# A language-model block on one core: another bracketing across chunks, the vector engine's first rows ahead of the router's choice, and a new order in the last stages of the first phase

## The reference, cut to what matters

```python
x = emb[tokens] * sqrt(256) + pos_enc            # per row of 256 tokens
h = softmax(q k^T / 16, axis=1) v
# mixer on u = layernorm(h): projections, 4-tap convolution, silu; 8 heads of 64, state 128, chunks of 128
Y_diag = einsum('bcln,bcsn,bhcls,bcshp->bclhp', Cc, Bc, Lm, Xc)
states = einsum('bcln,bhcl,bclhp->bchpn', Bc, decay_states, Xc)     # what a chunk leaves behind
Y_off  = einsum('bcln,bchpn,bhcl->bclhp', Cc, prev_states, exp(a_cs))
y = (Y_diag + Y_off + D * xs) * silu(z);  y = y * rsqrt(mean(y * y) + 1e-5) * norm_w
h = h + y @ out_proj_w.T + u
# router on layernorm(h): softmax, top 2 of 8 experts, a slot in its expert's 1024 rows for each choice
# experts: gelu(rows @ w1[e]) @ w2[e], weighted, added back to the tokens' rows
```

## Time and profile before

| | |
|---|---|
| median of 3 runs | 922.77 us (922.51 to 923.15) |
| the profiled execution | 922.38 us; its span in the trace 920.6 us |
| busy in the span | PE 902.8 (98%), DVE 633.6 (69%), ACT 528.5 (57%), POOL 512.1 (56%) |
| from 0 to 536.96 us | first phase |
| from 544.15 us | the experts' products, on PE |

### The profile page before, as it was taken

The page is one execution under the profiler, slowest core; times in us unless marked ns, Lnnn a source line. Parts: engine busy times, 40 slices in busy tenths (PEclk is TensorE's granted clock), DMA queues, the critical chain, the costliest instruction groups (busy, mean ns, idle before and its releaser), DMA issues. The chain is left out here.

```text
span 920.6 us, 17776 instructions
## 1 busy us (share of the span) xinstructions
PE 902.8 (98%) x5832; PEld 805.0 (87%) x5832; DVE 633.6 (69%) x1698; ACT 528.5 (57%) x1097; POOL 512.1 (56%) x498
## 2 busy tenths in 40 slices
PE   8999999999999999999999979999999999999998
PEld 7888888888888888888888879999999999999997
DVE  1587889888988898889889644646464646464642
ACT  1767776677667766777677344444444444343442
POOL 5656877887788778877685522232333223232353
PEclk9999999999999999999999999999999999999999
DMA  7940011001000000000000044334434343433221
GB/s 220 321 148 17 31 47 35 23 35 34 13 23 14 24 13 23 14 25 13 12 14 4 26 152 110 96 85 93 91 83 100 76 107 70 113 66 71 24 55 49
DMA packets 49398, 59.13 MB, mean 64 GB/s; under 512 B 6304, under 2 KB 44683, under 8 KB 49360
## 3 DMA queue, kind: packets, MB, share of 16 engines
q1 hardware_dynamic: 35920, 42.14, 14.3%
q0 software_dynamic: 13440, 16.50, 10.6%
HBM read 33.62 MB, written 30.67 MB: 70 GB/s over the span
## 5 line engine op out<-in xcount | busy, mean ns | idle before, releaser
L691 POOL DMA_INDIRECT out<-ye,tok_slot x56 | 97.8, 1747 | 247.6 <-DMA out<-ye,tok_slot 121.2
L975 ACT ACTIVATE hf<-bank 128x512 f32<-128x512 f32 x128 | 79.4, 620 | 188.6 <-PE bank L1816 188.6
L1425 DVE TENSOR_TENSOR h_lo<-hf,h_hi 128x512 fp32r<-128x512 f32 x128 | 88.6, 693 | 102.7 <-ACT h_hi L977 102.7
L1814 PE MATMUL bank<-w_hi,h_hi 128*128 128x256 f32 x512 | 146.3, 286 | 0.0
L1816 PE MATMUL bank<-w_hi,h_lo 128*128 128x256 f32 x512 | 145.0, 283 | 0.0
L1815 PE MATMUL bank<-w_lo,h_hi 128*128 128x256 f32 x512 | 145.0, 283 | 0.0
L1124 DVE SCALAR_TENSOR_TENSOR xc<-bank,cw,xc 128x253 f32<-128x253 f32 (+2 forms) x288 | 128.2, 469 | 1.5
L1814 PE MATMUL bank<-xe_hi,w_hi 128*128 128x512 f32 x256 | 99.9, 390 | 0.0
L1815 PE MATMUL bank<-xe_lo,w_hi 128*128 128x512 f32 x256 | 99.9, 390 | 0.0
L1816 PE MATMUL bank<-xe_hi,w_lo 128*128 128x512 f32 x256 | 99.8, 390 | 0.0
L1815 PEld LDWEIGHTS bank<-w_lo,h_hi 128*128 128x128 f32 x512 | 98.4, 192 | 0.0
(11 more groups left out here) (223 smaller groups left out, 2349.5 us busy)
## 6 DMA issues: line engine op xcount, KB each, us to landing
w_raw<-w SPq DMA_DIRECT2D x16, 1024.0 KB, 7.7
slots_dram<-zero_row SPq DMA_DIRECT2D x1, 8320.0 KB, 30.6
xe<-slots_dram SPq DMA_DIRECT2D x15, 520.0 KB, 4.5
out<-hb SPq DMA_DIRECT2D x16, 256.0 KB, 2.2
w_raw<-in_wT SPq DMA_DIRECT2D x2, 644.0 KB, 5.9
out<-zero_row SPq DMA_DIRECT2D x1, 1024.0 KB, 32.4
slots_dram<-rows,slot POOLq DMA_INDIRECT x64, 2.2
out<-ye,tok_slot POOLq DMA_INDIRECT x64, 3.8
```

The lines of the kernel that those rows point to most:

```text
L691: g.indirect_dma_start(out, bass.IndirectOffsetOnAxis(ap=tok_slot[q][:, j:j + 1], axis=0), ye[q][:, j, :], None, compute_op=ALU.add).then_ ...
L975: sc.activation(hf[m % 2][:, :], h_bank[i % H_BANKS][:, :], ACT.Gelu_apprx_tanh)\
L1425: vc.tensor_tensor(h_lo[:, m, :], hf[m % 2][:, :], h_hi[:, m, :].bitcast(F32), ALU.subtract)\
L1814: te.matmul(out_, hi, rhi, start=first_, stop=False)
```

## The change

1. **Across chunks.** Y_off is bracketed as (C1 B0^T) times decayed X0. `state_inputs` on PE makes the 128x128 product of B and C in place of a transpose of B; `chunk_state` becomes `across_chunks`, of the same shape, whose result is what `carried_y` reads; `from_state` on PE and `state` on ACT are gone.
2. **Order in a half with all three.** DVE: `carried_y`, `first_y` and `split_hT` stand ahead of `router_top`. PE: `choices_before` stands behind the first projection of channels. POOL: `skip_x` waits until DVE's second `decay_scores` is done.
3. **Drain.** `residual(t)` of DVE stands first; D times xs is added on PE by products with diagonal matrices (`skip_diag`, made once on POOL in the second half) into the same PSUM accumulation as `own_chunk`; `decayed_x` is on ACT, as eight operations of 64 columns; most of `keep_clock` is gone; the tail's router is behind the back's residual; the back's output projection is cut in pieces.
4. **Last half.** `describe_rows` is on DVE, so that POOL's eight scatters stand in one row; `choices_before` of the tail of the drain is here.
5. **Expert 0.** PE has 34 `keep_clock` before `part_done` and 12 behind it, where 38 stood before it, and 8 behind the transposes instead of 6. ACT makes both high parts of the rows, between its two halves of the weights; DVE makes both low parts.

```diff
@@ pool half @@
+                        second_root(t, p)
+                        pool.wait_ge(y_ready[q], y_ready.now(b, q, 1))
                         with_bias(Turn(b.reg, b.shift - 1), q)
-                        second_root(t, p)
                         gated_root(b, q)
...
                 if b:
+                    pool.wait_ge(m_ready[KD - 1][q], m_ready[KD - 1].now(b, q))
                     skip_x(b, q, 0)
                     skip_x(b, q, 1)
@@ act half, drain @@
                     end_decay(b, q)
+                    decayed_x(b, q)
                     carry_exp(b, q)
                     decay(b, q, 2)
                     decay(b, q, 3)
-                    late_rows(b, q)
-                    state(b, q)
+                    norm_2(t, p)
                     square(b, q, 0)
@@ dve half, drain @@
+                    residual(t, p, p)
                     mask_scores(b, q, p)
...
-                    residual_sum(t, p, p)
-                    first_y(b, q)
-                    carried_y(b, q)
-                    second_y(b, q)
-                    residual_norm(t, p)
+                    last_y(b, q)
                     mean_square(b, q)
-                    residual(b, q, p)
+                    residual_sum(b, q, p)
                     router_in(t, p)
+                    residual_norm(b, q)
                     router_top(t, p)
@@ dve half @@
                     decay_scores(b, q, 1)
+                if b:
+                    carried_y(b, q, bank[q][3])
+                    first_y(b, q)
+                if f:
+                    split_hT(f, p)
                 if t:
                     router_top(t, p)
                 if b:
-                    first_y(b, q)
-                    carried_y(b, q)
-                if f:
-                    split_hT(f, p)
-                if b:
                     second_y(b, q)
@@ pe @@
-                    te.transpose(bank[where][3][:, 0:P], xc[p][:, KI, 0:P], ident[:, :])
+                    te.matmul(bank[where][3][:, 0:P], xc[p][:, KI, 0:P], xc[p][:, KI + 1, P:2 * P], start=True, stop=True)
...
-                def from_state(r, p):
-                    pe.wait_ge(st_ready[p], st_ready.now(r, p))
-                    pe.wait_ge(decay_ready[p], decay_ready.now(r, p))
-                    te.matmul(bank[p][2][:, :], xc[p][:, KI + 1, P:2 * P], st[p][:, :], start=True, stop=True)\
-                        .then_inc(yo_psum[p], 1)
+                def skips(r, p, c):
...
+                    for m in range(KI):
+                        te.matmul((bank[p][YD_BANK[0]], bank[1 - p][3])[c][:, m * P:(m + 1) * P], xc[p][:, m, c * P:(c + 1) * P],
+                                  skip_diag[:, m, :], start=(m == 0), stop=False)
@@ pe, expert 0 @@
-            keep_clock(0, 38)
+            keep_clock(0, 34)
             pe.wait_ge(part_done, 1)
+            keep_clock(0, 12)
```

More of the change, by code:

```diff
@@ L388, in lm_block @@
         FILL = dict(t=4, scores=4, attend=5, hT=18, dt=8)
-        DRAIN = dict(rows=2, seg0=1, seg2=8, state=2, out=2)
-        LAST = dict(v2T=10, route=2, choices=9)
+        DRAIN = dict(rows=2)
+        LAST = dict(first=9, v2T=2, route=2, choices=9)
         PER_TURN = 2 * NG * KF
@@ L656, in half @@
                 if b:
+                    pool.wait_ge(m_ready[KD - 1][q], m_ready[KD - 1].now(b, q))
                     skip_x(b, q, 0)
                     skip_x(b, q, 1)
+                if b and not t:
+                    skip_matrices()
                 if not final:
@@ L837, in end_decay, with decayed_x @@
                 copy(edec[p][:, :], seg[p][:, 0, :, P - 1], edec_ready[p])
-            def late_rows(r, p):
-                act.wait_ge(xdt_ready[p], xdt_ready.now(r, p))
-                copy(xs[p][:, 1, :], bank[1 - p][2][:, :], xs_ready[p])
+            def decayed_x(r, p):
+                act.wait_ge(edec_ready[p], edec_ready.now(r, p))
+                act.wait_ge(xdt_ready[p], xdt_ready.now(r, p, 1))
+                for h in range(NH):
+                    at = slice(h * HD, (h + 1) * HD)
+                    ins = sc.activation(xdec[p][:, at], xdt[p][:, 0, at], ACT.Copy, scale=edec[p][:, h:h + 1])
+                ins.then_inc(xdec_ready[p], 1)
             def x_rows(r, p, c):
@@ L986, in experts @@
                                           scale=w_slot[1][:, j:j + 1]).then_inc(ye_ready, 1)
-            for m in range(CHUNKS):
+            for m in range(CHUNKS // 2):
                 high_weights(1, 0, m)
+            act.wait_ge(first_half, 1)
+            sc.activation(xe_hi[0][:, 0, :], x_bank[0][:, :], ACT.Copy).then_inc(first_high, 1)
             act.wait_ge(xeT_psum, 1)
             sc.activation(xe_hi[0][:, 1, :], x_bank[1][:, :], ACT.Copy).then_inc(first_high, 1)
+            for m in range(CHUNKS // 2, CHUNKS):
+                high_weights(1, 0, m)
             run_experts(sc.Fori, experts)
@@ L1195, in second_y, with last_y @@
                     own = back.mark(vc.tensor_tensor(y[p][:, 1, :], bank[p][YD_BANK[1]][:, :], y[p][:, 1, :], ALU.add))
+                    gated(r, p, 1, own)
+                def last_y(r, p):
+                    dve.wait_ge(yd_psum[p], yd_psum.now(r, p, 1))
+                    dve.wait_ge(sz_ready[p], sz_ready.now(r, p))
+                    vc.tensor_tensor(y[p][:, 0, :], bank[p][YD_BANK[0]][:, :], sz[p][:, 0, :], ALU.mult)\
+                        .then_inc(y_ready[p], 1)
+                    carried_y(r, p, bank[1 - p][1])
+                    back.wait(carried_y.last)
+                    dve.wait_ge(yd_psum[p], yd_psum.now(r, p))
+                    own = back.mark(vc.tensor_tensor(y[p][:, 1, :], bank[1 - p][3][:, :], y[p][:, 1, :], ALU.add))
                     gated(r, p, 1, own)
@@ L1341, in half @@
                     dt_in(f, p)
+                if not f:
+                    describe_rows(t, p)
                 if t:
@@ L1658, in to_yT, with project_rows @@
                         .then_inc(yT_psum[p], 1)
-                def project_rows(r, p, c, where):
+                def project_rows(r, p, c, where, ks=range(KI)):
                     pe.wait_ge(w_out_ready, 1)
                     pe.wait_ge(yT_ready[p], yT_ready.now(r, p, c + 1))
-                    for k in range(KI):
+                    for k in ks:
                         ins = te.matmul(bank[where][0][:, c * DM:(c + 1) * DM], yT[p][:, c, k, :], w_out[:, k, :],
                                         start=(k == 0), stop=(k == KI - 1))
-                    if c == KD - 1:
+                    if c == KD - 1 and ks[-1] == KI - 1:
                         ins.then_inc(out_psum[p], 1)
@@ L1729, in half @@
                 if not f:
+                    keep_clock(p, LAST["first"])
+                    choices_before(t, q)
                     keep_clock(p, LAST["v2T"])
                     to_v2T(t, p)
-                    choices_before(t, q)
                     keep_clock(p, LAST["route"])
@@ L1776, in half @@
                 if b:
-                    from_state(b, q)
-                if b:
                     own_chunk(b, q, 1)
-                if t:
-                    choices_before(t, p)
                 if b:
@@ L1788, in half @@
                     project_channels(f, p, 0)
+                if t:
+                    choices_before(t, p)
                 if nf:
```

119 lines of the change are left out of this document (64 added, 55 removed).

## The result

The changed kernel takes 925.34 us (median of ten executions, 924.17 to 925.62); the kernel before, run on the same chip, takes 922.62 (ten, 921.65 to 923.52). The ratio is 1.0029, with a 95% interval from 1.0019 to 1.0038: slower by 2.7 us or 0.3%, where I had forecast +1.0 us, within my range but on the slower side of 0.2%.

The account below looks back on a forecast made before the run. The prediction took the ring DVE, ACT, DVE to bound each half, with PE slightly ahead. Its terms, +5.5 - 0.9 - 2.7 - 0.9 = +1.0 us, gave 923.8 us in terms of the median; range 917.5 to 929.5.

Parts of the forecast that it names:

- The bound: First phase: DVE and ACT set the 30.87 us half; PE, though 99.8% busy, is 0.3 to 0.5 us ahead.
- the ring: In each half, the chain DVE, ACT, DVE, claimed to set the 30.87 us.
- Each half +0.39: Halves with all three parts: split_hT waits for hn, the router gets faster, dt_in comes at 304.61 instead of 304.22.
- By the rule `gated` takes the block instead: DVE in a half: gated (y times silu(z)), not the router's L1247, is held by POOL's skip_x; no separate size.
- 14 x 0.39 = +5.5: Fourteen halves with all three parts, each taken as 0.39 us longer: +5.5 us in all.
- Second half -0.9: Half without a tail: PE reaches the next batch's transposes 0.86 us earlier, then DVE is the bound: -0.9 us.
- Drain -2.7: Drain: slots 1.85 us sooner, and 0.6 to 1.1 from POOL's scatters in one row: -2.7 us, bounds -1.2 and -3.8.
- Expert 0 -0.9: Start of second phase: fillers keep PE's clock up, ACT and DVE share the split: -0.9 us, bounds 0 and -1.4.
- The order costs nothing: Rival, each half: DVE's wait for hT shrinks, 0 a half, total 918.3 us; chance 0.13.
- PE is the bound: Rival, first phase: all of 15 x 0.75 = 11.2 us on PE is gained, total 908; chance 0.10.
- The router stays blocked: Rival, each half: POOL holds L1247 at its new place, up to 0.93 us a half, wholly 936.8, half 930; chance 0.13.
- The lucky hole: Rival, the norm: DVE's lm and lv move ahead of POOL's with_bias, about a us a half, 908; chance 0.04.

Follow-up runs that it names:

- e4: Changed kernel plus one more 128x512 product on PE behind to_hT, into a bank nobody reads; 926.12 us, ratio 1.0035.
- e6: Changed kernel with router_top split on DVE: sums, maxima and indices between carried_y and first_y, cast and one-hots behind split_hT; 913.53 us, ratio 0.9899.
- e9: Changed kernel with router split, cast and one-hots behind split_hT, plus one unused 128x512 product on PE behind to_hT; 915.56 us, ratio 0.9922.
- e2: Kernel before with the order alone: router_top behind split_hT on DVE, choices_before behind the first project_channels on PE; 928.65 us, ratio 1.0066.
- e5: Changed kernel with the old order on DVE and PE, across_chunks at from_state's place; new bracketing, drain and expert 0 kept; 922.04 us, ratio 0.9993.
- e1: Changed kernel with router_top alone moved back ahead of carried_y, first_y and split_hT on DVE; 947.27 us, ratio 1.0271.
- e3: Changed kernel with router_top split on DVE: sums, maxima, indices and cast between carried_y and first_y, one-hots behind split_hT; 917.54 us, ratio 0.9953.
- e11: Changed kernel with the old fillers at the start of the second phase (38 ahead of part_done, none behind), timed; 926.78 us, ratio 1.0040.
- e10: Changed kernel with expert 0's first rows split by DVE alone again, new fillers kept, timed; 926.07 us, ratio 1.0034.

## Why the prediction was right, and where it was off

The median moved by +2.7 us where I had forecast +1.0. The direction is that of the sum, but to a slowing beyond 0.2% I had given no more than 0.34. Against the span, in the order of the sum (predicted, then read in the trace):

```text
start, to v of half 2            0        +0.45
second half                     -0.9      -0.65
halves 3 to 16, order           +5.5      +7.06   (6.76 to v of half 16, +0.3 to its dt_in)
drain                           -2.7      -2.87
expert 0                        -0.9      -0.83
sum                             +1.0      +3.16
```

- **The start** is no term of mine and hardly one of the change: across the traces v of the first half lies anywhere from 17.68 to 18.50. Without it the sum is +2.7, as the medians say.
- **The bound.** Right, and tested from both sides: 0.86 us more on PE changed no steady half of the changed kernel (e4), and 0.4 us less on DVE's way to `dt_in` than before gave 0.4 a half (e6). That PE had slack before too is made likely by e9: with one 128x512 product more than the changed kernel, as before the change, PE gets through a half in 30.62 us, 0.26 under the 30.88 of before, though in another order. Two things were too simple. PE's stretch from `gm` to `to_hT` is part of the ring; and PE's new waiting, foretold ahead of `attend` ("L1536's successor", which is L1560), came ahead of the segment sums that need `gm` (1.1 us a half, L1641), while the wait for v stayed at 5.2 us in 12.
- **Each half +0.39.** Right in its main mechanism, that the split must wait for hn, and near in size: 31.31 - 30.88 = 0.43. The order alone gave 0.34 in the kernel before (e2); the old order took it away (e5). DVE's split waited 0.41 us in most halves. What I had not seen is that `first_y` would wait 0.63 for `skip_x` by semaphore; I had only a later of two cases, in which an instruction is held up to the end of `skip_x`. By that case DVE reaches the split at about the same time, still ahead of hn, so the sum is the same: here a wrong detail cost nothing.
- **By the rule `gated` takes the block instead.** It did not: all 24 in the twelve halves took 0.69 us. It started at 302.49, when `skip_x` had 0.1 us to go, because `first_y` had waited.
- **The step that was mis-sized** is "14 x 0.39 = +5.5", in that it takes all fourteen halves as alike. Ten steps are (+0.43). The one from half 3 lost 0.86, of which 0.78 is the order's (31.50 in e2). Of what it lost beyond a steady half, 0.15 is that half 3 was the shorter one before: v to `dt_in` took 14.17 us in place of 14.32, and `oh` 0.19. The other 0.27 is idle time of DVE ahead of `second_y` at 86.61, which the steady halves don't have; what it waited for the profile doesn't show. And the step from half 15 to 16 lost 1.06. The rows of half 15, POOL and DVE:

```profile
455.96 1.20 POOL L566 TENSOR_TENSOR shift<-lnr,lnm 128x4 f32<-128x4 f32 x1 [0.18 <-POOL lnr L562]
```

```profile
455.88 1.23 DVE L1172 TENSOR_TENSOR seg<-seg,gm 128x1024 f32<-128x1024 f32 x1 [0.22 <-ACT seg L745]
...
460.93 0.69 DVE L1074 TENSOR_TENSOR hT_lo<-hn,hT_hi 128x512 fp32r<-128x512 f32 x1 [1.01 <-ACT hn L791]
```

  POOL's `shift`, which takes 0.20 us elsewhere (at 299.19, 0.04 ahead of DVE's scores at 299.23; only in the second half it takes 0.53, in both kernels), started 0.08 behind them here and took 1.20, to their end; ACT's hn and all that hangs on it came a us late. It is there in e1 (1.07 us), in e3, e4 and e6 to e11 (1.20 to 1.29), and not in the kernel before, where `shift` started 0.05 ahead of the scores, nor in e2 or e5. That this is why the half is longer is read from the traces; no run removed it.
- **Second half -0.9.** -0.65, and for another reason than the product less: DVE's wait for the transposes fell to 0.24 from 1.02, but its wait for hn grew from 0.32 to 1.01, and in e4 and e5 a product between `to_hT` and those transposes undid the gain.
- **Drain -2.7.** -2.87. ACT's eight operations of `decayed_x` took 2.02 us, taken as 2. The back's residual on DVE (`residual_sum`) came 41.42 us behind v of half 16, before 42.22: 0.80 sooner, foreseen 0.75, a number that the prediction's list of gains and losses doesn't add up to, so its fit is partly luck. The tail's first scatter came 47.71 us behind that v (529.21 - 481.50), before 49.71: 2.00, foreseen 1.85. One detail was wrong: the last batch's slots, begun at 533.92, were ready only as POOL finished the tail's scatters (534.13), not before, and the profile puts the 0.88 us ahead of the scatter at 535.01 down to them; the step between the groups was 0.82 before. From the first scatter to the last are 9.64 us, before 10.21, a gain of 0.57 at the low end of "0.6 to 1.1".
- **Expert 0 -0.9.** -0.83; the traces of e10 and e11 show both of its reasons at work, one execution each.
- **Rivals.** "The order costs nothing" and "PE is the bound" fell with e2 and e4. "The router stays blocked" fell: `oh` took 0.19. The clock stayed at 1.00 through the drain. The lucky hole did not come; its 908 doesn't follow from "about a us a half" either, which gives 923.8 - 14 = 909.8. Of what should show it, the last scatter was to come 1.9 us later than at 534.86, and came 4.0 later: the two uneven halves above and the start.

## What to carry to other kernels

An engine that is blocked by another's instruction is not a loss by itself: here the blocked time was spent while DVE would have had to wait for `skip_x` and hn anyway, and taking the block away only showed those waits. Before moving work away from a block, list what must still arrive behind it, and fill that time with work that the block doesn't touch; here this turned +0.3% into -1.0% with the same instructions. Extra work on an engine is free only off the chain: PE's extra product cost nothing behind `to_hT` in e4 and 0.16 us a half in e9, once the ring was shorter. And an order written for two engines moves on both or on none (e1).

## What the runs showed of the hardware

- A cast of four elements from one SBUF tensor to another is held while GpSimd's `skip_x` runs: 0.77 us in most halves of e3 (0.77 to 0.87 in all fourteen) against 0.16 to 0.17 in e6, where it stands behind `skip_x`. I had counted only operations with two SBUF inputs as exposed. The Trainium skill has it (SBUF — State Buffer, "Who interferes with whom": copies and casts can run in a two-port mode and then contend with GpSimd as well); the duration agrees, though no row shows the mode. The maxima and indices beside the same `skip_x` were not lengthened.
- The hold goes the other way too: GpSimd's `shift` took 1.20 in place of 0.20 us when it came 0.08 us behind DVE's scores (to their end), and 0.20 when it came 0.03 to 0.05 ahead of them. A shift of about 0.1 us decided about one us.
- Short waits of PE can go with a lower clock: one wait of 1.56 us in each half of some 33 (e1) went with a mean granted clock of 0.95 over three halves, where waits of 1.1 us in halves of 31.3 (the changed kernel) left it at 1.00.
